# One core of attention and FFN: the product with v on whole-height tiles, the heads' weights from ScalarE's queue, q and k in one broadcast

## What is computed

```python
# x: (64, 64, 512) float32; 64 samples of 64 tokens, 512 channels
h = einsum('bct,bcd->bdt', x, cond_weights[subjects])        # per sample 64x64, mixes the tokens
q, k, v = h @ Wq, h @ Wk, h @ Wv                              # 16 heads of 128 each
beta, gate = sigmoid(h @ Wb + bb), silu(h @ Wg)
q, k = [layernorm(silu(causal_dwconv(t, 4 taps))) for t in (q, k)]
S_t = (1 - beta_t) * S_{t-1} + beta_t * outer(v_t, k_t)       # scan over the 64 tokens
o_t = S_t @ q_t
x = x + (o * gate) @ Wo
x = x + ternary_ffn(x @ W2.T + adapter(x))                    # rank-16 adapter by sample, 8-bit rows, ternary weight
```

## Time and profile before

| | before |
|---|---|
| median of three runs | 2547.58 us |
| profiled execution, whole | 2545.06 us |
| profiled execution, span | 2543.3 us |
| instructions | 38355 |
| matmul records of TensorE | 14263 |
| mean granted TensorE clock | 0.984 |
| DMA: moved, mean rate | 551.38 MB, 217 GB/s |
| SyncE's DMA queue (q1), share of 16 engines' span | 62.6% |
| ScalarE's DMA queue (q10) | 2.4% |

### The profile page before, as it was taken

One profiled execution on the slowest core, in us unless ns is written; L12 is line 12 of the kernel. 1 busy time (PEld: TensorE's weight loads), 2 busy tenths in 40 slices (PEclk: granted clock), 3 DMA queues, 4 the chain that ended last, 5 costly groups with the idle time before them and its releaser, 6 DMA issues. The chain is left out here.

```text
span 2543.3 us, 38355 instructions
## 1 busy us (share of the span) xinstructions
PE 2444.2 (96%) x14263; PEld 1847.0 (73%) x14292; DVE 1625.5 (64%) x2653; ACT 1073.2 (42%) x1615; POOL 786.1 (31%) x636
## 2 busy tenths in 40 slices
PE   6889999999999999999999999999999999999996
PEld 5667777777777777777777777777777777777764
DVE  3666665676567666676556766667566676667663
ACT  4554543534444343443434434444344433444331
POOL 3465532232232222232233232232232232232241
PEclk9999999999999999999999999999999999999997
DMA  6788867576566776666676676666766577566660
GB/s 228 243 306 285 275 212 240 170 246 241 184 229 197 231 226 210 199 204 224 212 234 196 203 245 221 212 203 200 260 203 219 170 244 240 186 223 203 228 198 25
DMA packets 326962, 551.38 MB, mean 217 GB/s; under 512 B 98354, under 2 KB 122970, under 8 KB 326778
## 3 DMA queue, kind: packets, MB, share of 16 engines
q1 hardware_dynamic: 315778, 529.75, 62.6%
q10 hardware_dynamic: 11000, 19.18, 2.4%
HBM read 495.08 MB, written 53.74 MB: 216 GB/s over the span
## 5 line engine op out<-in xcount | busy, mean ns | idle before, releaser
L559 POOL TENSOR_TENSOR og_lo<-gt,og_hi 128x512 fp32r<-128x512 f32 x128 | 180.8, 1413 | 1105.2 <-ACT og_hi L1073 1105.2
L1143 PE MATMUL pj_a<-ht_hi,wg 128*128 128x512 f32 x1024 | 361.4, 414 | 16.0 <-DMA wg<-parts_g 12.7
L1143 PE MATMUL pj_a<-ht_hi,wq 128*128 128x512 f32 x1024 | 354.4, 407 | 7.2 <-issue 3.2
L837 DVE SCALAR_TENSOR_TENSOR y_q<-pj_a,conv,y_q 128x504 f32<-128x504 f32 (+2 forms) x384 | 281.1, 732 | 125.0 <-ACT y_q L1049 115.7
L1143 PE MATMUL pj_b<-ht_hi,wk 128*128 128x512 f32 x1024 | 346.3, 399 | 6.3 <-DMA wk<-parts_k 6.3
L1143 PE MATMUL ring<-wv,ht_hi 128*128 128x512 f32 x1024 | 319.8, 394 | 1.3 <-POOL wv L549 1.3
L837 DVE SCALAR_TENSOR_TENSOR y_k<-pj_b,conv,y_k 128x504 f32<-128x504 f32 (+2 forms) x384 | 281.4, 733 | 52.6 <-ACT y_k L1049 43.5
L555 POOL TENSOR_TENSOR y_k<-y_k,sq_k 128x512 f32<-128x512 f32 x128 | 171.7, 1342 | 457.8 <-DMA sq_k<-m_rows 457.2
L1143 PE MATMUL ring<-wo,og_hi 128*128 128x512 f32 x992 | 312.6, 396 | 0.0
L1143 PEld LDWEIGHTS pj_b<-ht_hi,wk 128*128 128x128 f32 x1024 | 192.1, 188 | 103.8 <-issue 49.5
L1143 PEld LDWEIGHTS pj_a<-ht_hi,wg 128*128 128x128 f32 x1024 | 198.5, 194 | 64.8 <-DMA wg<-parts_g 14.0
(11 more groups left out here) (198 smaller groups left out, 4649.5 us busy)
## 6 DMA issues: line engine op xcount, KB each, us to landing
wq<-parts_q SPq DMA_DIRECT2D x112, 512.0 KB, 4.2
wk<-parts_k SPq DMA_DIRECT2D x112, 512.0 KB, 6.3
wg<-parts_g SPq DMA_DIRECT2D x112, 512.0 KB, 6.0
wv<-parts_v SPq DMA_DIRECT2D x112, 512.0 KB, 6.5
wo<-parts_o SPq DMA_DIRECT2D x108, 512.0 KB, 6.6
sq_q<-m_rows SPq DMA_DIRECT2D x110, 256.0 KB, 3.6
sq_k<-m_rows SPq DMA_DIRECT2D x110, 256.0 KB, 4.5
sq_q<-r_rows SPq DMA_DIRECT2D x110, 256.0 KB, 3.5
```

The source lines that it names most:

```text
L559: G.tensor_tensor(og_lo[:, u % OG_RING, :], gt[:, u % GT_RING, :], og_hi[:, u % OG_RING, :].bitcast(F32), ALU.subtract).then_inc(S["oglo"], 1)
L837: V.scalar_tensor_tensor(out=yy[:, :, k:], in0=pp[:, :, :L - k], scalar=conv[:, i, h, 3 - k:4 - k], in1=yy[:, :, k:], op0=ALU.mult, op1=AL ...
L1143: last = T.matmul(psum, a, b, start=start and n == 0 and m == 0, stop=stop and n == len(pairs) - 1 and m == 2)
```

## The change

1. `attend` and `weigh`: a new tile `decay_bd` of 128 x 512 is set to zero once by GpSimd. `weigh` writes the weighted scores of each pair of samples as two diagonal blocks of a 128 x 128 block in it, in two operations (even samples' partitions, odd samples' partitions). `attend` makes four matmuls with all 128 rows and 128 moving columns, into the one ring bank. `gate_out` becomes one operation of 512 columns. `m0` is then free as soon as the scores are weighted: `score` and `scan` wait for `weighed` and no longer for `og_odd` and the product.
2. `load_head` moves from SyncE to ScalarE: q behind the first tap of q, k behind the first tap of k, g behind the gate's activation.
3. q and k of a unit share one tile `sq_both`, and the four broadcasts of 256 KB are two of 512 KB, each with one semaphore.
4. SyncE's loop: `send_means` comes ahead of the loads of the sets of Wv, Wo and W2 of that slot; the subjects' weights (`load_cond`) are loaded two samples a slot in four slots instead of eight in one.
5. `adapt` works in its ring bank and not in `xam`; the small tile `gamma_cols` moves into `acc`.

```diff
-        sq = {n: sb(f"sq_{n}", [P, 2, GROUP]) for n in "qk"}
+        sq_both = sb("sq_both", [P, 2, 2, GROUP])
+        sq = {n: sq_both[:, :, i, :] for i, n in enumerate("qk")}
+        decay_bd = sb("decay_bd", [P, GROUP])
...
+        def pair_rows(rows, u):
+            return rows[2 * u:2 * u + 2, :].rearrange("(o x) t -> o x t", o=1).broadcast_to([P, 2, GROUP])
...
-                for j in range(4):
-                    x_ = "qk"[j % 2]
-                    if m:
-                        sp.wait_ge(S[f"n_{x_}"], 2 * m - 1 + j // 2)
-                    sp.dma_start(sq[x_][:, j // 2, :], m_rows[j:j + 1, :].broadcast_to([P, GROUP])
-                                 ).then_inc(S[f"m_in_{x_}{j // 2}"], 16)
+                for u in range(2):
+                    for x_ in "qk" if m else "":
+                        sp.wait_ge(S[f"n_{x_}"], 2 * m - 1 + u)
+                    sp.dma_start(sq_both[:, u], pair_rows(m_rows, u)).then_inc(S[f"m_in{u}"], 16)
...
+                if U % 2 == 0 and ROWS_SP <= U <= UNITS:
+                    send_means(U // 2 - 1)
                 if g < GROUPS and h in (0, 4) and g * SETS + h // 4 >= SETS:
                     for part in range(SET):
                         load_v(g * SETS + h // 4, part)
...
-                if H <= U + 1 < UNITS:
-                    load_head("q", U + 1)
-                if U % 2 == 0 and ROWS_SP <= U <= UNITS:
-                    send_means(U // 2 - 1)
-                if H <= U + 1 < UNITS:
-                    load_head("k", U + 1)
...
-                if H <= U + 1 < UNITS:
-                    load_head("g", U + 1)
...
             def weigh(u):
                 dve.wait_ge(S["scores"], u + 1)
                 dve.wait_ge(S["scanned"], u + 1)
-                V.tensor_tensor(decay[:], m0[:, 0:HALF], decay[:], ALU.mult).then_inc(S["weighed"], 1)
+                if u:
+                    dve.wait_ge(*made("pv", u - 1))
+                else:
+                    dve.wait_ge(S["setup_pool"], 9)
+                for b in range(2):
+                    half = slice(b * L, (b + 1) * L)
+                    V.tensor_tensor(even_odd(decay_bd[half, :], b), m0[half, 0:HALF].rearrange("p (i t) -> p i t", t=L),
+                                    decay[half, :].rearrange("p (i t) -> p i t", t=L), ALU.mult).then_inc(S["weighed"], 1)
...
-                for b, bank_ in enumerate((ring_bank("pv", u, 0), m0)):
-                    th = even_odd(t, b)
-                    V.tensor_tensor(th, bank_[:, 0:HALF].rearrange("p (i t) -> p i t", t=L), th, ALU.mult
-                                    ).then_inc((taken_sem("pv", u), S["og_odd"])[b], 1)
+                V.tensor_tensor(t, ring_bank("pv", u, 0)[:], t, ALU.mult).then_inc(taken_sem("pv", u), 1)
...
                 if U < UNITS:
                     first_tap("q", U)
+                if H <= U + 1 < UNITS:
+                    load_head("q", U + 1)
...
                 if U < UNITS:
                     first_tap("k", U)
+                if H <= U + 1 < UNITS:
+                    load_head("k", U + 1)
...
                 if U < UNITS:
                     gate(U)
+                if H <= U + 1 < UNITS:
+                    load_head("g", U + 1)
...
-                for b in range(ROWS):
-                    at, cols = L * (b % 2), slice(b // 2 * L, (b // 2 + 1) * L)
-                    mm = T.matmul((ring_bank("pv", u, 0), m0)[b % 2][:, cols], v[at:at + L, s % 2, b // 2, j * P:(j + 1) * P],
-                                  decay[at:at + L, cols], start=True, stop=True)
+                for i in range(HT):
+                    cols = slice(i * P, (i + 1) * P)
+                    mm = T.matmul(ring_bank("pv", u, 0)[:, cols], v[:, s % 2, i, j * P:(j + 1) * P], decay_bd[:, cols],
+                                  start=True, stop=True)
```

More of the change, by code:

```diff
@@ L331, in load_x, with load_cond @@
                 sp.dma_start(acc[:, g % 2], x_rows[g].rearrange("i p d -> p i d")).then_inc(S["x_in"], 16)
-            def load_cond(g):
+            def load_cond(g, pair):
                 sp.wait_ge(*made("cond", g - 1, HT - 1))
-                for b in range(ROWS):
+                for b in (2 * pair, 2 * pair + 1):
                     subj = sp.value_load(subj_row[0:1, bass.ds(g * ROWS + b, 1)], min_val=0, max_val=cond_w.shape[0] - 1)
@@ L465, in _ @@
                 g, h = divmod(U, H)
+                if U == UNITS + 1:
+                    for part in range(SET):
+                        load_last_o(part)
+                if U == UNITS + 3:
+                    for part in range(SET):
+                        load_last_w2(part)
+                if U < H - 1:
+                    split_traffic(U)
+                if U % 2 == 0 and ROWS_SP <= U <= UNITS:
+                    send_means(U // 2 - 1)
                 if g < GROUPS and h in (0, 4) and g * SETS + h // 4 >= SETS:
@@ L474, in _ @@
                         load_w2(g - 1, part)
[L475 to L480, removed]
                 if h == 12 and 1 <= g < GROUPS:
@@ L1017, in send_means @@
                 act.wait_ge(S["mean_kept"], m + 1)
-                for j in range(4 if m else 0):
-                    act.wait_ge(S[f"m_in_{'qk'[j % 2]}{j // 2}"], 16 * m)
+                for u in range(2 if m else 0):
+                    act.wait_ge(S[f"m_in{u}"], 16 * m)
                 act.dma_start(m_rows, rstd[0:P:32, :]).then_inc(S["m_out"], 16)
@@ L1023, in spread_means @@
                 act.wait_ge(S["m_out"], 16 * (m + 1))
-                for j in range(4):
-                    x_ = "qk"[j % 2]
-                    if m:
-                        act.wait_ge(S[f"n_{x_}"], 2 * m - 1 + j // 2)
-                    act.dma_start(sq[x_][:, j // 2, :], m_rows[j:j + 1, :].broadcast_to([P, GROUP])
-                                  ).then_inc(S[f"m_in_{x_}{j // 2}"], 16)
+                for u in range(2):
+                    for x_ in "qk" if m else "":
+                        act.wait_ge(S[f"n_{x_}"], 2 * m - 1 + u)
+                    act.dma_start(sq_both[:, u], pair_rows(m_rows, u)).then_inc(S[f"m_in{u}"], 16)
             def send_rstd(m):
                 act.wait_ge(S["rr"], m + 1)
-                for j in range(4 if m else 0):
-                    act.wait_ge(S[f"r_in_{'qk'[j % 2]}{j // 2}"], 16 * m)
+                for u in range(2 if m else 0):
+                    act.wait_ge(S[f"r_in{u}"], 16 * m)
                 act.dma_start(r_rows, rstd[0:P:32, :]).then_inc(S["r_out"], 16)
@@ L1038, in spread_rstd, with load_head @@
                 act.wait_ge(S["r_out"], 16 * (m + 1))
-                for j in range(4):
-                    x_ = "qk"[j % 2]
-                    act.dma_start(sq[x_][:, j // 2, :], r_rows[j:j + 1, :].broadcast_to([P, GROUP])
-                                  ).then_inc(S[f"r_in_{x_}{j // 2}"], 16)
+                for u in range(2):
+                    act.dma_start(sq_both[:, u], pair_rows(r_rows, u)).then_inc(S[f"r_in{u}"], 16)
+            def load_head(name, u):
+                act.wait_ge(S[f"proj_{name}"], u)
+                if u == H:
+                    act.wait_ge(S[f"saved_{name}"], 16 * H)
+                act.dma_start(block_both(name, u % H), parts[name][u % H]).then_inc(S[f"w{name}_in"], 16)
             def first_tap(x_, u):
```

61 lines of the change are left out of this document (26 added, 35 removed).

## The result

The changed kernel takes 2486.18 us (median of 4 runs, 2484.63 to 2488.64), the kernel before 2546.39 us beside it (4 runs, 2544.25 to 2547.93): a ratio of 0.9765, with a 95% interval of 0.9748 to 0.9782, 60 us less. Forecast were 2489 us, with 2474 to 2518 as the range. The profiled execution of the changed kernel took 2486.88 us with a span of 2485.1; before, they were 2545.1 and 2543.3. All that follows compares spans, if nothing else is said.

What follows compares the result with a forecast made beforehand. TensorE, with matmuls in flight for 96% of the span, was taken as the bound. 2545.1 - 41 - 19 - 4 + 2 + 2 = 2485, plus 2.5 to the median and 1 for small waits: 2489 us, range 2474 to 2518.

Steps and rivals of the forecast that it cites:

- The product: Product with v on TensorE: stage falls from 1.24 to 0.92 us, 0.32 a head over 128 heads, 41 us saved.
- rival 1: Leaving the product with v costs as much as today: saving 14 us instead of 41, 2516 us; chance 0.14.
- Rival 3: Packing half-height tiles was worth its price: full matmuls at 0.23 pitch, 75 us more, 2604 us; chance 0.01.
- The waits for weights: TensorE's waits for `wg` (12.7 us) and `wk` (6.3) vanish when ScalarE issues the loads: 19 us saved.
- TensorE waited for none of this in the steady loop, so: 0: One broadcast for q and k, with sets issued behind the means on SyncE, costed at 0 us.
- 2 + 2: TensorE waiting for VectorE: +2 us around head 10 and after head 12, +2 us for weighted scores in the last slots.
- 0.13 us a group: Allowance in the slot after head 12, where the gate's activation must fit beside the product alone.
- Rival 5: VectorE bounds slots of heads 8 to 10 by 2 us more than allowed in seven groups: 2503 us; chance 0.09.
- about 2: SyncE's wait for `m_rows` falls from 4 us each to about 2, as a sign the prediction is right.
- The 4 us put on the clock: Extra saving of 4 us on TensorE, for the slow first matmul and lower granted clock behind long weight waits.
- rival 4: A set of weights lands late, in the slot of head 12: 2552 us; chance 0.03.
- rival 6: TensorE's waits for `y_q` shrink too, with shorter round trips: 10 us more gain, 2479 us; chance 0.12.

Runs made afterwards that it cites:

- B: Kernel before with only the product with v by four full-height matmuls of 128 columns (weigh, gate_out and adapter adapted): 2530.80 us, ratio 0.9948.
- H: Kernel before with only the heads' weights issued by ScalarE instead of SyncE: 2545.50 us, ratio 1.0003.
- P: Kernel before with only two broadcasts of 512 KB for q and k in place of four of 256 KB: 2537.52 us, ratio 0.9972.
- O: Kernel before with only SyncE's order changed, the sets behind the means and the k load: 2557.29 us, ratio 1.0039.
- H+O: Kernel before with heads' weights issued by ScalarE and means ahead of the sets; old product, four broadcasts: 2521.62 us, ratio 0.9906.
- B+P+O: Changed kernel with the heads' weights issued by SyncE again: 2508.38 us, ratio 0.986.
- B+H+P: Changed kernel with the sets ahead of the means again in SyncE's loop: 2493.72 us, ratio 0.979.
- B+H+O: Changed kernel with four broadcasts of 256 KB again and the subjects' weights in one slot: 2494.72 us, ratio 0.9795.
- The 64-column kernel: Changed kernel with the product with v as eight full-height matmuls of 64 moving columns instead of four of 128: 2587.66 us.

## Why the prediction was right, and which of its steps failed

All the parts in one table, as us against the kernel before beside it (medians; the intervals of the ratios are 4 to 9 us to either side):

| B | H | P | O | H+O | B+P+O | B+H+P | B+H+O | all |
|---|---|---|---|---|---|---|---|---|
| -14 | +1 | -7 | +12 | -24 | -36 | -51 | -52 | -60 |

**The product: right.** Entry, pitch and exit were read off neighbouring stages of the same shape. Forecast were 0.92 us for the stage, measured are 0.89; 41 us, measured 45. Taken as a whole the exit costs nothing (rival 1 falls): the first step behind the product is still slow, 0.31 us against 0.34 in the earlier trace rows and a plain 0.23, but the matmul ahead of it starts 0.81 us after the first record, sooner than eight pitches of 0.11. The 64-column kernel shows that the doubled columns aren't what is paid for, which the prediction had only concluded from equal pitches. Rival 3, that packing was worth its price, falls too. On the page TensorE: Matmul & The Clock Gate (Why this matters for your kernels), the Trainium skill advises row groups for a small contraction; for these tiles the trace disagrees that this pays, 1.24 us with them and 0.89 without.

**The waits for weights: the 19 us went as forecast, the reason was incomplete.** The prediction gave them to ScalarE's issuing alone and costed the broadcasts and the order at 0 each. That is the step that failed: "TensorE waited for none of this in the steady loop, so: 0". Being out of the list of waits only meant that the round trip was the second latest, not that it had room. H alone removes the 19 us and finds the variance waiting instead; O alone costs 12, since it makes `wg` later; together they give 24. P alone gives 7. Of the full change H is worth 24 us, P 8 and O 9, the last two at the edge of the noise. H and O are worth more together than apart, and the sum came out because both were there. It was also read that a set or a head's weights ahead in the queue made the round trip long; a head's weights alone don't: in the slots of head 8 before, with only `wq` issued 1.3 us ahead, it takes 2.0 to 2.3 us.

**The product's gain also hung on the loads.** The working added -41 and -19 as if independent. B alone keeps 14 of its 45 us. That the two terms could be added was right for the full change only, in which the loads had slack; no rival held this, and the profile before shows it: where a load ends a slot, a shorter stage in it gives nothing.

**VectorE: right in place, mis-sized.** The slots of head 10 and the last ones were named. `weigh` is 418 ns for each half and `gate_out` 688, as costed, and busy time rose by 31 us (35 forecast). But in the slot of head 10 TensorE now waits in each of the seven groups, 0.76 us for a quantized tile and 0.38 for the weighted scores, 8.0 us in all; before it had 2.5 there, in three of the groups. The waits for the weighted scores at the end grew from 1.6 to 5.2. That is 9.1 us more where 2 + 2 were allowed. Not all of it is the new product's: H and O together, with the old one, have 0.59 a group for the tile, a wait that the one for `wg` had hidden. In the slot of head 13 the forecast 0.13 us a group was not paid (16.59, the plain slot 16.57), in that of head 12 0.14 was (16.71). Rival 5, which asked for 2 us more in each group, did not come. The 5 us that VectorE cost too much and the 4 us that the product gave too much nearly cancel, which is luck. (The wait for q's taps, 3.1 to 5.5, lies in the first group almost whole, and P alone has it too, 5.6.)

**The rest.** SyncE's wait for the means went from 220.6 to 133.3 us in 55, 2.4 each, where "about 2" was said. It didn't get shorter everywhere: in the slots of head 10 the round trip still takes 7.1 to 8.1 us, since a set goes out at the end of the slot before. In the changed kernel the write and the broadcast of the round trip in a slot of head 8 stand 2.20 us apart, with nothing ahead of them:

```profile
1646.76 0.53 SPq L361 DMA_DIRECT2D m_rows<-rstd  x1
1648.96 0.81 SPq L366 DMA_DIRECT2D sq_both<-m_rows  x2
```

The 4 us put on the clock fit the trace. Behind waits for weights, two slots of the steady groups ran at a lower granted clock before (head 3 once, 23.27 us at 0.85; head 10 once, 21.91 at 0.92), and none does in the changed kernel. The first is 6.3 us above a plain slot and holds 3.7 of wait, which leaves 2.6; for the second the same comparison with its neighbours leaves about 1.4, an estimate. (The 0.50 us that the prediction took from the earlier trace rows as the undisturbed first matmul is a q projection's; the gate projection's has 0.50 as well.) No set came late (rival 4). The wait for `y_q` shrank by 3.4 us, a third of what rival 6 hoped for. The profiled execution lies 0.7 us above the median here, not 2.5 below it.

**What stays open.** Whether the means' return is slow behind a set because both share SyncE's queue or because both share the DMA engines isn't told apart: no kernel sent the sets from a third queue. Kernels with the heads' weights or the sets in a tight place scatter more (27 us between the ends for H alone, 4 us for the changed kernel), and none of the runs shows what tips them.

## What to carry to other kernels

Cost a stage by the starts of its neighbours in the timeline, and look for the new shape elsewhere in the same trace: that gave 45 us to within 4. When a wait is taken away by taking a transfer out of a queue, look at what else was in this queue and only a little earlier, and cost it by its room, not by its absence from the list of waits; the parts of such a change can be worth 0 and +12 alone and -24 together. And a stage that gets shorter gives its gain only in slots that no transfer ends; the work moved behind an engine's wait for DRAM inherits that wait whole.

## What the runs showed of the hardware beyond what was expected

- Float32 records with 128x128 weights start 0.11 us apart with 64 moving columns as with 128 (16 records in 1.70 us, eight in 0.81, the last one overlapped by what follows). Pairs of half-height records of 64 columns took 0.12: two tiles at once at the price of one, and no better than the one twice their size.
- Changing from float32r matmuls of full height to float32 ones and back costs little (0.23 into it, as a plain step, and 0.31 for the first step behind); into half-height tiles and back it was 0.32 and 0.34.
- An 8 KB write with its return took 7.5 to 9.8 us behind a set of 2 MB in the same queue while another queue loaded too (H alone, head 6), and 2.0 to 2.3 us with nothing right ahead of it (changed kernel, head 8).
- Slots of the same work took 20.06 and 20.83 us at a granted clock of 1.00 and 21.65 to 21.96 at 0.92 (B alone, head 10, waits of 1.9 to 2.8 us in each).
